# Gathers moved into the last attention steps of a mixture-of-experts layer, with the layer's drain, weight loads and residual sums rearranged

## The reference

```python
def _L0_attn_ref(x, ...):            # 16 heads of 8; keys: the top 30% (76) of 256 tokens by an importance
    _, top_idx = jax.lax.top_k(importance, k)
    ...
    attn = jax.nn.softmax(scores, axis=-1)
    out = jnp.einsum('bhqk,bhkd->bhqd', attn, V)
    return out @ wo.T + bo

def _L0_ffn_ref(x, wg, w1, w3, w2):   # 8 experts; each takes its 512 best tokens of 4096
    scores = jax.nn.softmax(xt @ wg, axis=-1)
    top_scores, sel = jax.lax.top_k(scores.T, CAPACITY)
    routed = xt[token_idx] * top_scores.reshape(-1, 1)
    h = jax.nn.silu(routed @ w1) * (routed @ w3)
    routed_out = h @ w2
    out = jnp.zeros_like(xt).at[token_idx].add(routed_out)
```

## Time and profile before

| | |
|---|---|
| median of 3 runs | 2335.9 us (2333.53 to 2336.21) |
| the profiled execution | 2334.09 us |
| its span, first to last instruction | 2332.3 us |
| TensorE busy | 2103.5 us, 90% |
| VectorE, ScalarE, GpSimd busy | 1467.2, 1126.0, 898.8 us |
| mean granted TensorE clock | 0.945 of full speed |

### The profile page before, as it was taken

The page is one execution under the profiler, slowest core; times in us unless marked ns, Lnnn a source line. Parts: engine busy times, 40 slices in busy tenths (PEclk is TensorE's granted clock), DMA queues, the critical chain, the costliest instruction groups (busy, mean ns, idle before and its releaser), DMA issues.

```text
span 2332.3 us, 48280 instructions
## 1 busy us (share of the span) xinstructions
PE 2103.5 (90%) x16208; PEld 1565.6 (67%) x16224; DVE 1467.2 (63%) x4256; ACT 1126.0 (48%) x3600; POOL 898.8 (39%) x1417
## 2 busy tenths in 40 slices
PE   5787957289999999999999899999988999999998
PEld 2564624267777777777777666666666777777776
DVE  6988923256665666666556655555556777777776
ACT  3543323144444444454444445555455655655654
POOL 3113153534444444444444411111114444544544
PEclk8977869689999999999999899999998999999999
DMA  6000015420000000000000000000000000000001
GB/s 191 2 1 1 2 39 148 93 81 1 1 2 1 2 2 2 2 1 2 2 2 1 1 1 0 0 0 0 0 0 2 1 2 2 2 2 2 2 2 37
DMA packets 37334, 36.89 MB, mean 16 GB/s; under 512 B 5632, under 2 KB 34432, under 8 KB 36352
## 3 DMA queue, kind: packets, MB, share of 16 engines
q1 hardware_dynamic: 31488, 29.82, 4.0%
q0 software_dynamic: 5632, 4.33, 1.3%
HBM read 23.53 MB, written 10.62 MB: 15 GB/s over the span
## 4 chain that ended last, share of the span: by engine, by line
PE 68%; DVE 5%; ACT 4%; issue 3%; POOL 1%; DMA 1%; POOLq 0%; DVEq 0%; SPq 0%; ACTq 0%
PE bank L1301 8%; PE bank L1290 6%; PE bank L1227 5%; PE bank L1276 5%; PE bank L1273 4%; PE bank L1323 4%; PE bank L1270 3%; PE bank L1212 3%; PE bank L1214 2%; PE bank L1213 2%; PE bank L1293 2%; PE bank L1688 2%; PE bank L1710 2%; PE bank L1712 2%; PE bank L1711 2%
## 5 line engine op out<-in xcount | busy, mean ns | idle before, releaser
L1584 POOL TENSOR_TENSOR work<-work 128x128 f32<-128x128 f32 (+1 forms) x1048 | 503.9, 513 | 740.2 <-DVE work L1484 740.2
L1362 ACT ACTIVATE work<-bank,work 128x128 f32<-128x128 f32 x524 | 192.4, 367 | 621.6 <-DVE work L1473 621.6
L1479 DVE COPY work<-bank 128x384 f32<-128x384 f32 x520 | 282.3, 548 | 31.7 <-PE bank L1301 4.2
L1363 ACT ACTIVATE work<-bank,work 128x256 f32<-128x256 f32 x524 | 247.9, 473 | 0.0
L1301 PE MATMUL bank<-w_const,work 128*128 128x128 f32 x1560 | 227.5, 282 | 0.4 <-POOL work L1584 0.4
L1472 DVE TENSOR_REDUCE work<-bank 128x1 f32<-128x128 f32 x524 | 149.9, 286 | 110.0 <-PE bank L1276 101.7
L1473 DVE TENSOR_REDUCE work<-bank 128x1 f32<-128x256 f32 x524 | 217.5, 415 | 0.1
L1505 DVE COPY work<-bank 128x512 f32<-128x512 f32 x136 | 94.0, 692 | 163.2 <-PE bank L1222 156.5
L1301 PEld LDWEIGHTS bank<-w_const,work 128*128 128x128 f32 x1560 | 165.7, 141 | 45.5 <-issue 38.9
L1290 PE MATMUL bank<-work 128*64 128x256 f32 x1032 | 169.0, 405 | 0.3 <-DVE work L1505 0.3
L1381 ACT ACTIVATE work<-bank 128x512 f32<-128x512 f32 x266 | 162.5, 611 | 7.9 <-PE bank L1214 7.7
(11 more groups left out here) (339 smaller groups left out, 4978.1 us busy)
## 6 DMA issues: line engine op xcount, KB each, us to landing
w_l<-in_l SPq DMA_DIRECT2D x1, 3210.5 KB, 10.4
w_l<-in_l SPq DMA_DIRECT2D x1, 3080.0 KB, 13.7
w_f<-in_f SPq DMA_DIRECT2D x1, 3072.0 KB, 13.9
x_sb<-in_x SPq DMA_DIRECT2D x4, 512.0 KB, 6.0
normed_rows<-work SPq DMA_DIRECT2D x1, 2048.0 KB, 9.3
even_experts<-x_sb SPq DMA_DIRECT2D x8, 256.0 KB, 3.6
residual<-x_sb SPq DMA_DIRECT2D x1, 2048.0 KB
qk<-in_qk SPq DMA_DIRECT2D x2, 1024.0 KB
```

Of the source, the lines that this page charges most:

```text
L1363: act.activation(pr[g % 4][:, Q1], scored(i, g)[:, Q1], ACT.Exp, bias=nmx[:, g % 4, 1:2], accum_out=sm[:, g % 4, 1:2]).then_inc(s_ex.s, 1)
L1479: dve.tensor_copy(pt[g % 4], PS[2 + g % 2][:, 0:384]).then_inc(s_te.s, 1)
L1584: ins = pool.tensor_tensor(w, w, spread(rc[:, g % 4, q:q + 1], w.shape[1]), ALU.mult)
```

## The change

- The one-hots come eight to a half step instead of four (`OH_STEPS` = 2), in steps 10 and 11, and `list_index` stands in step 12.
- GpSimd issues the gathers of two experts in each of the steps 12 to 15, in place of all 32 after step 15. The second expert of a step waits for the first half of the next step's scores (in step 15 for the heads of sequence 14).
- The drain stands in another order on TensorE and VectorE.
- Layer 1's weights are loaded after the first, second and fourth expert's result, those in `l1` in two halves with a semaphore each; `qk1` has a semaphore of its own.
- VectorE makes all four residual sums.

```diff
-LOADS = (("const",), ("l0",), ("f0",), ("l1",), ("l2", "l3"), ("qk1", "qk3", "masks"))
+LOADS = (("const",), ("l0",), ("f0",), ("l1",), ("l2", "l3"), ("qk1",), ("qk3", "masks"))
...
-        OH_FROM, OH_EACH, OH_BUFS = 10, 4, 8
+        OH_FROM, OH_STEPS, OH_EACH, OH_BUFS = 10, 2, 8, 8
...
+            def gathered(e):
+                if e >= 3:
+                    pool.wait_ge(b_got[e % 3], 16 * CT * (e // 3))
+                for t in range(CT):
+                    pool.indirect_dma_start(xg[:, CT * e + t, :], None, rows_d, slot(e, t)).then_inc(b_got[e % 3], 16)
...
                 if t == LIST_STEP + 1:
                     list_words()
-            pool.wait_ge(b_idx, 1)
-            pool.wait_ge(rows_out, 48)
-            for e in range(E0):
-                if e >= 3:
-                    pool.wait_ge(b_got[e % 3], 16 * CT * (e // 3))
-                for t in range(CT):
-                    pool.indirect_dma_start(xg[:, CT * e + t, :], None, rows_d, slot(e, t)).then_inc(b_got[e % 3], 16)
+                if t == OH_FROM + OH_STEPS:
+                    pool.wait_ge(b_idx, 1)
+                    pool.wait_ge(rows_out, 48)
+                if t >= OH_FROM + OH_STEPS:
+                    gathered(2 * (t - OH_FROM - OH_STEPS))
+                    if t + 1 < B:
+                        pool.wait_ge(a_s, 2 * t + 3)
+                    else:
+                        pool.wait_ge(a_o, B - 1)
+                    gathered(2 * (t - OH_FROM - OH_STEPS) + 1)
...
             dve.wait_ge(a_A, B)
+            scaled(0)
             heads_normed(B - 2)
-            scaled(0)
+            scaled(1)
             added(B - 2)
-            scaled(1)
             heads_normed(B - 1)
...
-            for c in (0, 1, 2):
+            for c in range(4):
...
-            pool.wait_ge(acc_in, 16)
-            pool.wait_ge(x_back[3], 16)
-            pool.tensor_tensor(x_sb[:, 24:32, :], x_sb[:, 24:32, :], acc_back[:, 3072:4096].rearrange("p (t d) -> p t d", d=D), ALU.add)
...
+            sp.wait_ge(b_y, 1)
             sp.dma_start(qk_raw["qk1"], ins["qk1"]).then_inc(w_in["qk1"], 16)
-            sp.dma_start(regions["l1"][:, :], ins["l1"]).then_inc(w_in["l1"], 16)
+            sp.wait_ge(b_y, 2)
+            sp.dma_start(regions["l1"][:, 0:width("l1") // 2], ins["l1"][:, 0:width("l1") // 2]).then_inc(l1_half, 16)
+            sp.wait_ge(b_y, 4)
+            sp.dma_start(regions["l1"][:, width("l1") // 2:], ins["l1"][:, width("l1") // 2:]).then_inc(w_in["l1"], 16)
             sp.dma_start(masks_raw, ins["masks"]).then_inc(w_in["masks"], 16)
...
-            output(B - 2)
             pe.wait_ge(a_sub, 2 * B)
             turn(0)
-            weights_turned(B - 1, range(8))
+            weights_turned(B - 1, range(4))
+            output(B - 2)
+            weights_turned(B - 1, range(4, 8))
+            turn(1)
             heads(B - 1)
-            turn(1)
             pe.wait_ge(w_in["f0"], w_all["f0"])
             up(0)
             output(B - 1)
```

24 lines of the change are left out of this document (13 added, 11 removed).

## The result

The changed kernel took **2307.5 us** (median of 4 runs, 2305.69 to 2311.24), the kernel before 2334.7 beside it: ratio **0.9885, 95% interval 0.9868 to 0.9903**. It is faster, as forecast, by 27 us instead of 52, and lies 1.5 us above the range (2272 to 2306). The profiled execution was the longest of the four, 2311.24 us with a span of 2309.4, so 27.0 us over the forecast's 2284.2.

The account below looks back on a forecast made before the run. GpSimd's queue of 32 gathers, then 32 scatters, was taken as the frame, with VectorE full ahead and a slow TensorE patch. Terms -4.5 + 2 - 38.5 - 3 - 5.9 = -49.9 gave 2284 us from 2334.1; range 2272 to 2306.

Parts of the forecast that it names:

- B: From T to the first scatter: -38.5 us, of which -34.2 from escaping the patch and -4.3 from the drain's new order.
- A: Steps 10 to 15, with doubled one-hots and steps 12 and 13 at 13.0 us each: -4.5 us, bounds -6 and +3.
- the patch: Slow TensorE stretch during the gathers after step 15, cause unnamed; early gathers were expected to remove most of its 34.2 us.
- T: End of VectorE's last subtraction, in step 15: 310.9 before, forecast at 306.4.
- the patch also meets steps 12 and 13: Rival: 5 us more in each of these steps and a later drain, +21 to +35, about 2310; chance 0.12.
- The allowance of 2: +2 us in steps 12 to 14, because GpSimd's gathers and blocks fill 12.7 of 13.0 us, a cover of 0.3.
- C: The scatters: spreading layer 1's loads over four results leaves the first two scatters more room, -3 us, bounds 0 and -6.
- D: The close: GpSimd's drain instruction no longer ends last, so layer 1 starts earlier, -5.9 us, bounds -1.1 and -6.
- slower: Rival: the patch costs TensorE 1.7 us for each of all 32 gathers plus four recoveries, +71, 2353; chance 0.04.
- Blocks late: Rival: gathers slowed beside VectorE in steps 12 to 14 delay GpSimd's key blocks, +11 replacing the allowance, 2293; chance 0.07.
- The supply of instructions: Alternative reading of the patch: gathers slow TensorE's instruction supply beyond its queue of 64, giving the rivals' sum.

Follow-up runs that it names:

- after_again: The kernel after, unchanged, on the fifth chip, where the kernel before took 2305.1 us: 2285.9 us.
- late_gathers: The kernel after with all 32 gathers behind step 15 again: 2320.5 us, ratio to before 0.9942.
- spread_paced: The kernel after with four gathers in each of steps 12 to 15, sixteen behind, and a 0.54 us GpSimd instruction behind each: 2290.4 us, ratio to before 0.9809.
- after_beside: The kernel after, unchanged, on a further chip where the kernel before took 2336.1 us profiled: 2308.4 us, ratio 0.9884.
- paced_third: spread_paced unchanged, on the second of two more chips, where the kernel before took 2334.6 us: 2293.3 us.
- paced_beside: spread_paced unchanged, on the same chip as after_beside: 2290.2 us, ratio to before 0.9809.
- after_paced: The kernel after, still eight gathers to a step, with a 0.54 us GpSimd instruction behind each, on the fifth chip: 2288.6 us.

## Why the prediction was right and wrong

**The step that failed** is in B and in A: that the gathers cost TensorE nothing where they lie beside steps 12 to 15 and the first 12 us of the drain ("Without the patch, `heads` of sequence 14 starts 0.7 us after T", and 13.0 us for steps 12 and 13). The patch was taken to be something of the place behind step 15, because 56 matmuls beside the first seven gathers had run at pace. What came was the rival "the patch also meets steps 12 and 13", to which I had given 0.12 and a time of about 2310. The forecast was 27.0 us short of the profiled execution, in these terms:

- T +13.9: step 12 +4.7, step 13 +6.7, step 14 +1.0, the rest +1.5 (9.3 us from the start of step 15 to T for 7.8).
- `heads` of 14 at T + 13.9 for T + 4.4: +9.5. `heads` started at T + 6.8 and not T + 0.7, after waits of 4.03, 1.79 and 1.55 us on TensorE, and then both halves ran at the lower clock (granted 0.50; 3.64 us each, 1.93 and 1.91 in after_again).
- From there to the first scatter 25.2 us for 24.0: +1.2.
- Scatters and close 82.5 us for 81.0: +1.5.
- The allowance of 2 was in the forecast and is contained in what was measured, -2; and behind layer 1's start +2.9, which is run to run.

The 4.7 of step 12 lie ahead of the gathers (see A), the rest of T and `heads` go with them. late_gathers, spread_paced and after_again show it, each in its own way: take the gathers out of the steps, put them 1.66 us apart, or go to the other chip, and steps 13 and 14 take 13.1 us. What goes with the gathers is thus 6.7, 1.0, 1.5 and 9.5 of the above, 18.7 us in all; on one chip the paced kernel took 18.2 less than the kernel after. With after_again nearly every number of the forecast stands: T 309.0 (306.4), heads of 14 at T + 4.6 (T + 4.4), first scatter at T + 28.2 (T + 28.4), scatters 65.2 (64.5), time 2285.9 (2284.2). That doesn't make it right: the sum took the patch away in the drain and at no cost elsewhere, and on that chip there was, by the kernel before's 2305.1, no patch to take away; the gain is 19, not the 52 that I forecast. It is in part luck, too: T is 2.6 us later than forecast, and the allowance of 2, which nothing used up, covers it.

**A.** Where nothing is late, the doubled one-hots bring T from 311.0 to 309.4 or 309.0, -1.6 to -2.0, and not -4.5. Step 11 took 23.8 us (23.0). The largest error is in step 12, 14.3 instead of 13.0: I moved VectorE's batches and did not count that TensorE's product of one-hots doubles as well and that the last of them falls in this step; the cause is read from the kernel, no run varies it. In the result's run step 12 took 3.3 us more than in late_gathers: the granted clock was 0.50 from 255 to 265 and 0.59 from 265 to 270, against 0.82, 0.50 and 1.00 in the same three stretches of late_gathers. That part is run to run: step 12 took 14.7 in after_beside, which is the same kernel, and 17.7 in paced_third against 14.3 in paced_beside. The forecast had no term for it.

**B, the order of the drain.** -4.3 forecast, -4.6 measured by itself.

**C.** The later loads: -3 forecast, not shown. The stage took 67.5 us before and 66.7 after in the result's run, 62.4 to 69.3 in the ten runs with the old loads and 63.7 to 66.9 in the nine with the new ones.

**D.** -5.9 forecast, -6.5 in the profile (22.4 us to 15.9), -6.8 by itself.

**The sums.** 32 scatters with their gaps are 59.5 us, not 59.7. The range's lower end of 2272 doesn't follow from A and C at their lower bounds, which give 2279.7, or 2277.7 without the allowance. The point at which the rival "slower" begins is 1.1 us a gather and not 1.6, if the 16 us for four recoveries are counted as they are in its 71. None of this moves the result out of or into the range.

**Blocks late.** Beside a busy VectorE the gathers took 0.94 to 1.10 us in every run, but for the first one of each (1.30 to 1.36), so they weren't slowed. (A calculation of GpSimd's does go with a slower VectorE: in the kernel after, L483 took 1.25 us at 274.24, beside the value blocks, and 0.26 us at 276.65, beside a gather.) The rule of the Trainium skill, GPSIMD Engine Reference, Specifications, that stood behind this rival is not seen in any gather of these runs; after_paced shows what a full GpSimd queue does.

**The supply of instructions.** The rule of the Trainium skill, Advanced Engine Details and Errata, Engine Queue Depths, led to the time that came (about 2310), and it can't be put aside. In the patch of the kernel before the rows look like a slow supply: after some 36 matmuls with their weight loads at pace, the next ones start 0.70 or 1.40 us behind the last, with no semaphore between them. The rows after show another thing: ScalarE and VectorE wait for signals of matmuls that had long been issued and, by their rows, were done. Whether both are one effect, no run tells. One form of the rival the trace speaks against: the DMA packets that carry instructions (16 KB each, queue q8) are as fast in the patch as ahead of it, 0.91 us for the one at 322.0 and 0.93 to 1.32 for the five from 263 to 300.

**What stays open.** Why gathers by index hold back TensorE's instructions and signals, why that fades as they are put further apart, and why one chip of five showed none of it. Whether the profiler has a part in it is open as well: every run on record has a span and a granted clock, which speaks for the profiler recording in all of them, none is known to be without it, and its records of semaphores are incomplete in just the stretches with gathers by index. Other things than the chip may have changed with it, such as where the program and its memory were put; I had no way to vary them. The kernel before has no profile on that chip: that its patch is absent there follows from its time, 2305.1, close to the 2302.5 with plain transfers elsewhere, and is argued, not shown.

## What to carry to other kernels

When a slow stretch has no cause in the trace, moving what lies beside it is a bet: price it as if the slowness moved along, and ask first how each instruction behaves if the neighbour is spaced out or replaced. A pause of half a microsecond on an idle GpSimd behind each gather was worth, with the gathers spread over the drain, 18 us on top of the 26 that the whole change gained there, and nothing in an account of busy time would have proposed it. And where a time differs by over a per cent from chip to chip, find out on which kind a gain was measured before it is believed: this change gave 26 to 27 us where the kernel before takes 2334 to 2336, and 19 where it takes 2305.

## What the runs showed that I had not expected

- On four of five chips TensorE was held back while gathers by index were issued every 1.25 us: in the kernel before its instructions started 0.70 or 1.40 us apart, and in the kernel after the semaphores that it raises came up to 3.4 us late (normally 0.01 to 0.05). Put 1.66 us apart, the gathers left no signal over 0.6 us late. Scatters by index, 1.87 us apart, did nothing of the kind (0.01 us at most between 377 and 445 in the kernel before).
- As many plain transfers through the same queue, issued by GpSimd in 17.2 us, disturbed nothing.
- In the stretches with gathers by index on those four chips some rises of semaphores are missing from the trace, of TensorE, ScalarE and VectorE (7 of TensorE's 52 in the kernel after, 10 of 72 in spread_paced, where hardly one is late). A rise paired with the wrong end looks like a late signal, so count both sides first.
- On the fifth chip, in four runs, no signal of TensorE was over 0.06 us late from 200 to 450 and no rise is missing; one of them, after_again, had the same gathers at the same distance.
- The kernel before took 2333 to 2336 us on four chips and 2305.1 on the fifth, while the kernel after spent 1866.4 and 1867.4 us from layer 1's start on, on the one kind and on the other.
